# Window attention with a routed FFN: tile transfers over 128 partitions, and another order of z in memory

## What is computed

```python
x = x + _L0_conv_ref(_ln_c(x), qkv_w, lepe_w, bias_table)      # shifts 0 and 2, both halves
t = t + _L0_ffn_ref(_ln_t(t), router_w, router_b, expert_w, expert_b)
```

## Time and profile before

| | us |
|---|---|
| three runs: median (lowest to highest) | 3484.97 (3475.89 to 3493.27) |
| the profiled execution | 3467.97 |
| its span, first to last instruction | 3466.1 |
| TensorE busy with matmuls | 3080.1 (89%) |
| GpSimd / VectorE / ScalarE busy | 2501.0 / 2229.3 / 1620.3 |
| mean granted TensorE clock | 0.943 of full speed |
| DMA | 517.72 MB, 149 GB/s over the span |

### The profile page before, as it was taken

One profiled execution on the slowest core, in us unless ns is written; L12 is line 12 of the kernel. 1 busy time (PEld: TensorE's weight loads), 2 busy tenths in 40 slices (PEclk: granted clock), 3 DMA queues, 4 the chain that ended last, 5 costly groups with the idle time before them and its releaser, 6 DMA issues.

```text
span 3466.1 us, 202400 instructions
## 1 busy us (share of the span) xinstructions
PE 3080.1 (89%) x84772; PEld 1797.6 (52%) x84772; DVE 2229.3 (64%) x4807; ACT 1620.3 (47%) x3362; POOL 2501.0 (72%) x4998
## 2 busy tenths in 40 slices
PE   4899998989989898988889989989889999999996
PEld 2555555555555455554555545555455555555552
DVE  2566666666666666676666667666666666666675
ACT  2554444444444454444445444444444445454541
POOL 4887767767777677777767777777677777777760
PEclk7999999999999899999999999999999999999997
DMA  2456565555656565565556555555555565656555
GB/s 63 109 136 168 145 160 140 160 145 149 160 140 165 140 160 147 146 160 139 159 150 156 153 153 154 155 149 149 149 149 158 150 162 152 168 152 165 156 147 156
DMA packets 447180, 517.72 MB, mean 149 GB/s; under 512 B 120976, under 2 KB 415376, under 8 KB 446096
## 3 DMA queue, kind: packets, MB, share of 16 engines
q1 hardware_dynamic: 280336, 390.69, 41.4%
q0 software_dynamic: 165888, 113.57, 13.2%
HBM read 312.67 MB, written 77.86 MB: 113 GB/s over the span
## 4 chain that ended last, share of the span: by engine, by line
PE 64%; SPq 10%; issue 9%; DMA 9%; DVE 4%; ACT 4%; DVEq 0%; ACTq 0%
PE bank L622 15%; PE bank L707 11%; PE bank L687 10%; PE bank L607 7%; DMA z<-fin 3%; SPq L501 3%; PE bank L713 3%; PE bank L647 3%; PE bank L727 3%; PE bank L660 3%; SPq L531 3%; DMA gate_rows<-gateT 2%; PE bank L721 2%; PE bank L732 2%; PE bank L746 2%
## 5 line engine op out<-in xcount | busy, mean ns | idle before, releaser
L575 POOL DMA_DIRECT2D vx<-vt x3072 | 1555.6, 515 | 458.1 <-PE bank L713 446.1
L563 POOL DMA_DIRECT2D kx<-k_sb x1536 | 737.1, 488 | 419.0 <-issue 268.7
L707 PEld LDWEIGHTS bank<-probT,vx 128*32 128x32 f32 x36864 | 607.9, 150 | 438.2 <-issue 393.9
L622 PE MATMUL bank<-kx,qx 32*32 32x64 f32 x36864 | 705.3, 226 | 107.3 <-issue 79.9
L622 PEld LDWEIGHTS bank<-kx,qx 32*32 32x32 f32 x36864 | 597.5, 111 | 387.8 <-issue 374.2
L707 PE MATMUL bank<-probT,vx 128*32 128x16 f32 x36864 | 672.2, 210 | 139.7 <-issue 126.8
L939 DVE TENSOR_TENSOR gx<-gate_wide,yn_pair 128x768 f32<-128x768 f32 x384 | 365.6, 953 | 463.3 <-DMA gate_wide<-gate_rows 293.6
L796 ACT ACTIVATE prob<-prob 128x512 f32<-128x512 f32 x576 | 360.3, 626 | 267.1 <-DVE prob L951 253.4
L687 PE MATMUL bank<-halo,conv_w 128*64 128x380 f32 (+6 forms) x2592 | 460.3, 482 | 1.1 <-issue 1.1
L951 DVE TENSOR_TENSOR prob<-bank,row_max 128x512 f32<-128x512 f32 x576 | 398.5, 692 | 16.7
L946 DVE TENSOR_REDUCE row_max<-bank 128x32 f32<-128x512 f32 x576 | 382.7, 664 | 38.1 <-PE bank L622 30.0
(11 more groups left out here) (72 smaller groups left out, 2969.7 us busy)
## 6 DMA issues: line engine op xcount, KB each, us to landing
gate_wide<-gate_rows SPq DMA_DIRECT2D x768, 192.0 KB
vx<-vt POOLq DMA_DIRECT2D x3072, 12.0 KB
halo<-xn SPq DMA_DIRECT2D x160, 240.0 KB
kx<-k_sb POOLq DMA_DIRECT2D x1536, 24.0 KB
z<-fin SPq DMA_DIRECT2D x192, 192.0 KB, 5.7
yn_pair<-yn POOLq DMA_DIRECT2D x384, 96.0 KB
xa<-in_x SPq DMA_DIRECT2D x192, 96.0 KB, 4.3
xn<-xa SPq DMA_DIRECT2D x192, 96.0 KB
```

The lines of the kernel that those rows point to most:

```text
L563: pool.dma_start(kx[to + m:to + C:4, r % 2, m, :], k_sb[at + m:at + C:4, r % 2, :])\
L575: pool.dma_start(vx[to:to + TOK, r % 2, col:col + 13:4, odd, :], vt[at:at + TOK, r % 2, x::2, :, :].rearrange("p h n k -> p h (n k)"))\
L622: last = MM(bank_s[r % 2][at, w * KEYS:(w + 1) * KEYS], qx[at, kr % 2, win, :, :].rearrange("p a i -> p (a i)"), kx[at, kr % 2, :, win * T ...
L707: last = MM(bank_o[32 * c:32 * c + 32, at * TOK:(at + 1) * TOK], vx[:, kr % 2, :, at % 2, at // 2 * 4 + ba], probT[:, kr % 2, at, ba * TOK ...
```

## The change

- `xa`, `xn`, `xt` and `out` move a whole tile in one DMA of 128 partitions. The DRAM side is walked by `halves`: two blocks (the tile's halves, 1,536 bytes apart), in each 64 channels, in each one run of 1,536 bytes.
- z is stored with plain and rolled alternating row by row. To have the rolled heads in the order in which the tile wants them, they are placed one pair further in the attention's layout; the tables (`ones`, `wq`, `wk`, `wv`, `bias`) and the column of `vx` that a piece of v goes to (line 574) follow. No instruction on TensorE, ScalarE or GpSimd is added, removed or given another size by this.
- `z0t` is loaded by one DMA of 128 partitions; so is `z2t`, except in the tile at an image's top edge (`t == 0`), where it comes in three DMAs of 64 partitions.
- `load_tile` (lag 33) keeps `xt` and the wait for `y_third`. The z loads, with their two waits for `z_stored`, become the step `load_z` at lag 35, so they come behind parts three and four of `spread_gates` and behind `load_halo`.
- The semaphore `tile_loaded` becomes `xt_loaded` (waited for by `y_first`) and `z_loaded` (waited for by `y_second`).

SP issues 24 DMAs per tile in place of 34. The core of the diff:

```diff
-        "ones": (g[:, None] == o32 // 16 * 2 + o32 // 2 % 2) & (p[:, None] // TOK % 2 == o32 % 2),
+        "ones": (g[:, None] == o32 % 2 * 2 + o32 // 4 % 2) & (p[:, None] // TOK % 2 == o32 // 2 % 2),
...
-                a, b, y = m // 4, m // 2 % 2, m % 2
+                at = (m + 2 * roll) % HEADS
+                a, b, y = at // 4, at // 2 % 2, at % 2
...
+            def halves(flat, im, t):
+
+                return flat[im][:, :, t * 2 * SPX:(t + 1) * 2 * SPX].rearrange("b c (f n) -> f (b c) n", f=2)
+
             def load_x(r, im):
-                for half in range(2):
-                    at = (r % IMT * (2 * SP) + half * SP) * W
-                    sp.dma_start(xa[half * C:(half + 1) * C, r % 2, :],
-                                 x_flat[bass.ds(im, 1)][:, :, at:at + SPX].rearrange("b c n -> c (b n)"))\
-                        .then_inc(x_loaded[r % 2], 16)
+                sp.dma_start(xa[:, r % 2, :], halves(x_flat, bass.ds(im, 1), r % IMT)).then_inc(x_loaded[r % 2], 16)
...
                 if ti := s.tile("load_tile"):
                     k, r = ti
+                    if s.later(r, 2):
+
+                        wait_alone(sp, y_made, k - 1)
+                    sp.dma_start(xt[:, r % 2, :], halves(xt_flat, bass.ds(s.image(r, IMT), 1), (r + 1) % IMT))\
+                        .then_inc(xt_loaded[r % 2], 16)
+                if ti := s.tile("load_z"):
+                    k, r = ti
...
                     for p in range(2):
                         wait_alone(sp, z_stored[p], counts[p] * 16)
...
-                    for half in range(2):
-                        put_x(half)
-                        put_z(z0t, half, 0, 0, 0, 4, 0, t * (2 * SP) + half * SP, SP)
-
-                    put_rolled(0, 0, (t * (2 * SP) + H - ROLL) % H, ROLL)
-                    put_rolled(0, ROLL, t * (2 * SP), SP - ROLL)
-                    put_rolled(1, 0, t * (2 * SP) + SP - ROLL, SP)
+                    z_of = z.rearrange("b (m l) n -> l b m n", l=2)
+                    sp.dma_start(z0t[:, r % 2, :], halves(z_of[0], im, t)).then_inc(z_loaded[r % 2], 16)
...
+                    if t == 0:
+                        put_rolled(0, 0, H - ROLL, ROLL)
+                        put_rolled(0, ROLL, 0, SP - ROLL)
+                        put_rolled(1, 0, SP - ROLL, SP)
+                    else:
+                        at = (t * (2 * SP) - ROLL) * W
+                        sp.dma_start(z2t[:, r % 2, :], z_of[1][im][:, :, at:at + 2 * SPX].rearrange("b c (f n) -> f (b c) n", f=2))\
+                            .then_inc(z_loaded[r % 2], 16)
...
                 if yt := s.tile("y_second"):
                     k, r = yt
+                    dve.wait_ge(z_loaded[r % 2], z_loads_to(s, r) * 16)
                     dve.wait_ge(y_step, k * 2 + 1)
```

More of the change, by code:

```diff
@@ L65 @@
     turn_p=19, product=20, divide=23,
-    store_z=24, load_halo=29, load_tile=33, conv=34, y_first=37, y_second=38, y_third=38, tile_sum=39, tile_variance=40, router=41, logits=44,
+    store_z=24, load_halo=29, load_tile=33, load_z=35, conv=34, y_first=37, y_second=38, y_third=38, tile_sum=39, tile_variance=40, router=41, logits=44,
     take_logits=44, gates=45, gap_exp=46, turn_gates=47, pair_yn=47, store_gates=48, spread_gates=49,
@@ L220, in lay_tables @@
             for m in range(HEADS):
-                a, b, y = m // 4, m // 2 % 2, m % 2
+                at = (m + 2 * roll) % HEADS
+                a, b, y = at // 4, at // 2 % 2, at % 2
                 for part, name in ((0, "wq"), (1, "wk")):
-                    put(name, rows, g * CH + a * 16 + h * 4 + m % 4, qkv_w[part * CH + h * HEADS + m])
-                here = (h - 1) % HD if roll and a and b else h
+                    put(name, rows, g * CH + a * 16 + h * 4 + at % 4, qkv_w[part * CH + h * HEADS + m])
+                here = (h - 1) % HD if roll and at < 2 else h
                 put("wv", rows, g * CH + h * 8 + y * 4 + b * 2 + a, qkv_w[2 * CH + here * HEADS + m])
@@ L374, in halos_to, with z_loads_to @@
             return s.image(r, IMT) * 14 + (last // 2 + 1) * 2 + (2 if last >= IMT - 2 else 0)
+        def z_loads_to(s, r):
+            last, per_image = r % IMT, IMT + 2 * (r % 2)
+            return s.image(r, IMT) * per_image + (last // 2 + 1) * 2 + (2 if last == IMT - 1 else 0)
         def per_row(flat):
@@ L384, in metaformer_block @@
         N_SPREAD_CLEARED = 2
-        XS_DMAS, TILE_DMAS, K_DMAS, V_DMAS, GATE_DMAS = 5, 10, 8, 16, 2
+        XS_DMAS, K_DMAS, V_DMAS, GATE_DMAS = 5, 8, 16, 2
         block = ctx.enter_context(nc.Block())
@@ L411, in slot @@
                     if r % IMT == 2:
-                        wait_alone(sp, xn_stored[r % 2], k // 2 * 32)
+                        wait_alone(sp, xn_stored[r % 2], k // 2 * 16)
                     load_x(r, s.image(r, IMT))
@@ L419, in slot @@
                     im = bass.ds(s.image(r, IMT), 1)
-                    for half in range(2):
-                        at = (r % IMT * (2 * SP) + half * SP) * W
-                        sp.dma_start(xn_flat[im][:, :, at:at + SPX].rearrange("b c n -> c (b n)"),
-                                     xa[half * C:(half + 1) * C, r % 2, :]).then_inc(xn_stored[r % 2], 16)
+                    sp.dma_start(halves(xn_flat, im, r % IMT), xa[:, r % 2, :]).then_inc(xn_stored[r % 2], 16)
                 if ti := s.tile("load_strips"):
@@ L427, in slot @@
                     if r % IMT == 0:
-                        wait_alone(sp, xn_stored[r % 2], (k // 2 + 1) * 32)
+                        wait_alone(sp, xn_stored[r % 2], (k // 2 + 1) * 16)
                     if r % IMT < IMT - 1:
-                        wait_alone(sp, xn_stored[(r + 1) % 2], ((k + 1) // 2 + 1) * 32)
+                        wait_alone(sp, xn_stored[(r + 1) % 2], ((k + 1) // 2 + 1) * 16)
                     if s.later(r, 2):
@@ L485, in slot @@
                         wait_alone(sp, z_stored[p], counts[p] * 16)
-                    if s.later(r, 2):
-                        wait_alone(sp, y_made, k - 1)
                     t = (r + 1) % IMT
                     im = bass.ds(s.image(r, IMT), 1)
[L492 to L503, removed]
-                    def put_rolled(half, at, row, rows):
-                        put_z(z2t, half, 1, 1, 0, 3, at, row, rows)
-                        put_z(z2t, half, 1, 0, 3, 1, at, row, rows)
@@ new lines, in put_rolled @@
+                    def put_rolled(half, at, row, rows):
+                        sp.dma_start(z2t[half * C:(half + 1) * C, r % 2, at * W:(at + rows) * W],
+                                     z_of[1][im][:, :, row * W:(row + rows) * W].rearrange("b c n -> c (b n)"))\
+                            .then_inc(z_loaded[r % 2], 16)
[6 more added lines that the diff above has]
+                        sp.dma_start(z2t[:, r % 2, :], z_of[1][im][:, :, at:at + 2 * SPX].rearrange("b c (f n) -> f (b c) n", f=2))\
+                            .then_inc(z_loaded[r % 2], 16)
@@ L538, in slot @@
                     im = bass.ds(s.image(r, IMT), 1)
[L539 to L542, removed]
+                    sp.dma_start(halves(out_flat, im, t), y_out[:, r % 2, :]).then_inc(out_stored[r % 2], 16)
             pipeline(sp, slot)
             for p in range(2):
-                sp.wait_ge(out_stored[p], N_TILE // 2 * 32)
+                sp.wait_ge(out_stored[p], N_TILE // 2 * 16)
         @block.gpsimd
@@ L573, in slot @@
                                 to, at = g * CH + x * TOK, g * CH + odd * TOK
[L574 to L575 removed]
+                                col = (g % 2 * 2 + x) * 2 + g // 2
+                                pool.dma_start(vx[to:to + TOK, r % 2, col:col + 25:8, odd, :],
                                                vt[at:at + TOK, r % 2, x::2, :, :].rearrange("p h n k -> p h (n k)"))\
@@ L717, in slot @@
                     k, r = ti
-                    pe.wait_ge(x_loaded[r % 2], (k // 2 + 1) * 32)
+                    pe.wait_ge(x_loaded[r % 2], (k // 2 + 1) * 16)
                     if s.later(r, 2):
@@ L976, in slot @@
                     k, r = yt
-                    dve.wait_ge(tile_loaded[r % 2], (k // 2 + 1) * (TILE_DMAS * 16))
+                    dve.wait_ge(xt_loaded[r % 2], (k // 2 + 1) * 16)
                     if s.later(r, 4):
```

6 lines of the change are left out of this document (3 added, 3 removed).

## The result

The changed kernel takes **4216.02 us** (median of four runs, 4207.42 to 4219.84) against 3484.39 for the kernel before, a ratio of 1.2096 with an interval of 1.206 to 1.2132: 21% slower. The profiled execution took 4219.84.

The account below looks back on a forecast made before the run. SP's queue bounds the kernel, TensorE close behind; after the change two DMA engines do: 91 tiles × 42.2 us = 3,840, plus 286, less 29, plus 2, times 1.0049, gives 4,120 us; range 3,900 to 4,600.

Parts of the forecast that it names:

- What bounds the kernel before: Loop before, 35.5 us per tile: SyncE's full queue sets the pace, TensorE's limit within some 2 us of it.
- The faster rival: Merged transfers spread over all 16 or enough engines, so SP's relief counts: 80 us gained, 3,405 us; chance 0.07.
- Two blocks outermost confine a transfer to two engines, always the same: Six merged transfers: each runs on the same two engines as xs, 4.2 us each, 25.1 us per tile.
- no difference: Two engines differ from transfer to transfer; landings 2 to 4 us longer eat SP's gain: 3,470 to 3,500 us; chance 0.03.
- The pair's load is the pace: In the loop, two engines stay busy and set the pace at 42.2 us per tile.
- ends of 40.0 and 44.4: Pair's work per tile, with the evenly spread rest costing 10.7 us at 23.5 GB/s or 15.1 by busy time.
- some 21 us for the pair today: Same count of work per tile on these two engines in the kernel before, so no limit shows there.
- The total: Whole kernel: 91 tiles at 42.2 us plus 286 around them, less 29, scaled to the median: 4,120 us, 18% slower.
- Slower still: Pair full and landings chained through xs, value, xn: 38 to 48 us per tile; 4,830 us at 50; chance 0.12.
- SyncE's relief of 11 us: SP's queue loses about 11 of 35 us per tile: 6.4 from fewer issues, 5.0 from z's wait.
- The new wait at `y_second`: VectorE waits for the later z there; costs nothing while 12.7 us suffice for transfers landing in 4 to 6.
- TensorE idle near 10 us per tile: Sign of being right: in the loop TensorE idles about 10 us per tile while the two engines set the pace.

Follow-up runs that it names:

- run 4: Kernel before with only the z loads moved to lag 35, nothing merged: 3383.98 us, ratio 0.9712.
- run 1: Changed kernel with all six merged transfers cut in two, z's order and later z loads kept: 3390.94 us, ratio 0.9738 to the kernel before.
- run 11: Changed kernel with x's four transfers cut in two and z0t, z2t merged with 128 rows outermost: 3385.39 us, ratio 0.9723.
- run 7: Changed kernel with z stored strip by strip, so z0t and z2t have 128 rows outermost; x's four transfers stay merged: 3647.41 us.
- run 2: Changed kernel with xt alone cut in two: 3863.72 us.
- run 3: Changed kernel with xn's store alone cut in two: 3947.68 us.
- run 5: Changed kernel with xs's 62-channel pieces cut into 48 and 14, taking xs off the pair: 4050.7 us.
- run 6: Changed kernel with z0t and z2t cut in two, the four transfers of x still merged: 3692.03 us.
- run 8: Changed kernel with the z loads put back at lag 33, all six transfers merged: 4214.26 us.
- run 12: Kernel of run 6 with the wait for the gates and the whole tail one slot later: 3695.31 us.

## Why the prediction was right

- **What bounds the kernel before**: right. With z's wait taken away, SyncE waits for engines and TensorE is 91% busy (run 4). The faster rival's price, 3,405 us, was near what it costs when its condition holds: 3,384 to 3,391 (runs 1, 4, 11). The prediction left half of 2.1 us per tile to edges and turns; the gain was 100 us, 1.1 per tile. That the fewer issues share in it was not so.
- **Two blocks outermost confine a transfer to two engines, always the same**: shown by the stretch with two transfers open, by 6.35 us for one store, by the two parts in which each lands, and by run 7. The rivals "faster" and "no difference" fail here.
- **The pair's load is the pace**: 42.2 us per tile against 42.65 measured. Runs 2, 3, 5 and 6 each give time by taking load off the pair wherever it is, and run 8 gives none by adding a wait. How full the pair is can be counted from the packets of SyncE's queue, from 400 us after the start to 400 us before the end. In the changed kernel exactly two are open 48% of the time and fewer than two 8%; before it was 14% and 18%, in run 1 6% and 30%. So the pair is nearly full and not quite. In runs 6 and 12 exactly two are open 37% and 35% of the time, fewer 10% and 12%. The single prices are less good: for 3.7 us of load taken off, the gain was 3.87 (`xt`), 2.95 (`xn`), 1.8 (xs) and 2.9 each (z). The sum stood between ends of 40.0 and 44.4, from what the pair does besides; at the upper end, 15.1, and with 5 × 4.2 + 2 × 0.5 of merged load, run 6 would be at 37.1, and it has 42.65 − 5.8, 36.9. One term sized so fits run 6 but puts the changed kernel 1.7 too high. So the total was better than its terms, and why the gains fall short is open: the rest of the load, or x's path taking over. The prediction's some 21 us for the pair today leaves out that z0t's 4 and z2t's 3 blocks would lie on it too, by its own reading some 3 us more; the sum doesn't use it.
- **The total**: the mis-sized terms were the ends, 4218.0 − 3881.2 = 337 us where 286 were carried over from before (the landings of filling and emptying are longer too), and 0.45 us per tile. With the 29 us taken off for the top edges, the 91 tiles come out 70 us and the ends 51 us above the sum. The scaling to the median took back 25, as this profiled execution lay above its median and not below: 96 us in all, the gap from 4,120 to 4,216.
- **Slower still**, by landings in a chain: not at 50 us per tile. Run 3 speaks against it for the changed kernel.
- **SyncE's relief of 11 us**: the wait of 5.0 went, and the merged issue is 0.6, as estimated from bounds of 0.40 and 1.26. But the z loads were to cost 0.8 to 2.5 us, and took 0.58 + 5.34 in the tile above. The step that failed is that an issue's cost was taken as fixed. It didn't change the time here: in run 8 these stalls are nearly gone and the time is the same.
- **The new wait at `y_second`**: 31.4 us in all over 96 tiles. Nothing, as said.
- **TensorE idle near 10 us per tile**: 9.3, as said. SyncE's long waits are for `gate_rows` and `xn`, two of the three named.

## What to carry to other kernels

Count the outermost blocks of both sides of a transfer before merging two: the merged one saved one issue of 0.6 us and cost 4.2 us of landing, and six of them on one pair of engines made 21%. The mean DMA share did not warn of it, as it fell from 0.57 to 0.47 while two engines filled; look for a stretch with one or two transfers open and read the engines from share times 16, or count the parts in which a transfer lands. Where a queue stands still for its own store, move the load that waits a few slots on: here that alone was 2.9%.

## What was not expected of the hardware

- **An issue can stall.** In the changed kernel the issue of `z2t` takes 5.44 us in the median, and a z store behind it took 3.55, against 0.40 to 0.62 for the other single issues shown above. A full pair alone doesn't do it: `z0t`, issued just ahead, takes 0.54 to 0.59 every time, and in run 8, where the time is the same, `z2t` takes 0.52 in the median. What decides it is open.
- **A transfer over all engines is as late as its slowest part.** The z store, dealt out over all engines, lands after 8.6 us in the page's median (5.7 before), though 14 of its 16 parts are there within 2. The read-back of the gates lands after 7.4:

```profile
gate_wide<-gate_rows SPq DMA_DIRECT2D x768, 192.0 KB, 7.4
...
z<-fin SPq DMA_DIRECT2D x192, 192.0 KB, 8.6
```

- **TensorE's clock fell as its idle time rose**: a mean of 0.864 of full speed against 0.943, with TensorE busy 77% of the span and not 89%, and the same 84,772 matmuls took 3238.9 us in place of 3080.1. TensorE idles in every tile and is 5% of the chain that ended last, so little of this is on the path.
